# A transformer layer on eight cores: attention in half-row head units braided with its norms, no barriers, and a guarded second form of the softmax

## What is computed

```python
x = x + attn(layernorm(x))          # x: 8192 x 2048
x = x + ffn(layernorm(x))

def attn(q_in):                     # H=16 heads, D=128, M=1024 stored patterns per head
    proj = rms_norm(q_in, norm_query_w) @ W_in.T
    q = proj.reshape(B, S, H, D) @ W_q.T
    k = stored_patterns @ W_k.T
    v = stored_patterns @ W_v.T
    scores = einsum('bshd,hmd->bhsm', q * sigmoid(beta), k)
    out = einsum('bhsm,hmd->bshd', softmax(scores), v)
    return rms_norm(out.reshape(B, S, H * D), norm_retrieved_w) + q_in

def ffn(x):                         # 2048 -> 8192 -> 2048, int8 weights
    fuse = silu((x @ w_gate) * s_gate) * ((x @ w_up) * s_up)
    return (fuse @ w_down) * s_down
```

## Time and profile before

| | us |
|---|---|
| three runs | 2159.86, 2160.74, 2166.98 (median 2160.74) |
| span of the profiled execution, slowest core (6) | 2165.7 |
| spans of the eight cores | 2147.5 to 2165.7 |
| PE busy | 1804.8 (83%) |
| ACT / DVE / POOL busy | 607.3 / 240.3 / 146.6 |
| mean granted TensorE clock of core 6 | 0.891 |

### The profile page before, as it was taken

The page is one execution under the profiler, slowest core; times in us unless marked ns, Lnnn a source line. Parts: engine busy times, 40 slices in busy tenths (PEclk is TensorE's granted clock), DMA queues, the critical chain, the costliest instruction groups (busy, mean ns, idle before and its releaser), DMA issues.

```text
span 2165.7 us, 20546 instructions; the slowest of 8 cores (2147.5 to 2165.7 us)
## 1 busy us (share of the span) xinstructions
PE 1804.8 (83%) x8488; PEld 839.3 (39%) x8488; DVE 240.3 (11%) x455; ACT 607.3 (28%) x596; POOL 146.6 (7%) x239
## 2 busy tenths in 40 slices
PE   2349958888841499999999999999997979899695
PEld 2224433443421244444444444444443434344242
DVE  3530000000038300000000000000000020100202
ACT  1351156556656211111111111111113212222120
POOL 1000010000002100000000000000000010000101
PEclk9559958888865699999999999999998989999898
DMA  7610050000024222222222222222213131221301
GB/s 164 151 20 1 0 78 1 1 1 1 1 97 165 88 78 78 78 78 78 78 78 78 73 70 72 78 78 78 78 59 102 39 102 39 78 64 39 99 23 58
DMA packets 42367, 142.06 MB, mean 66 GB/s; under 512 B 6181, under 2 KB 6182, under 8 KB 38950
## 3 DMA queue, kind: packets, MB, share of 16 engines
q0 software_dynamic: 28592, 96.58, 15.4%
q1 hardware_dynamic: 13686, 44.19, 6.3%
HBM read 103.10 MB, written 16.78 MB: 55 GB/s over the span
## 4 chain that ended last, share of the span: by engine, by line
PE 78%; ACT 7%; DVE 6%; DMA 5%; issue 3%; POOL 0%; DVEq 0%; ACTq 0%; POOLq 0%; SPq 0%
PE PS L936 21%; PE PS L951 20%; PE PS L1076 19%; PE PS L462 5%; PE PS L547 3%; PE PS L562 2%; DMA out<-arena 2%; ACT arena L591 2%; PE PS L611 1%; DMA arena<-patT 1%; DVE arena L323 1%; PE PS L584 1%; PE PS L578 1%; ACT arena L439 1%; ACT arena L386 1%
## 5 line engine op out<-in xcount | busy, mean ns | idle before, releaser
L1076 PE MATMUL PS<-arena 128*128 128x512 bf16 x1956 | 451.9, 386 | 55.0 <-DVE arena L1015 44.3
L936 PE MATMUL PS<-arena 128*128 128x512 bf16 x2048 | 455.1, 381 | 5.6 <-DMA arena<-wu 5.6
L951 PE MATMUL PS<-arena 128*128 128x512 bf16 x1984 | 438.7, 379 | 0.0
L1076 PEld LDWEIGHTS PS<-arena 128*128 128x128 bf16 x1956 | 193.5, 99 | 298.1 <-issue 75.2
L936 PEld LDWEIGHTS PS<-arena 128*128 128x128 bf16 x2048 | 200.8, 98 | 249.2 <-issue 9.1
L951 PEld LDWEIGHTS PS<-arena 128*128 128x128 bf16 x1984 | 194.3, 98 | 234.0
L960 ACT ACTIVATE arena<-PS,sgc_s 128x1024 bf16<-128x1024 f32 x64 | 71.3, 1114 | 735.5 <-PE PS L945 735.5
L1043 ACT ACTIVATE arena<-arena 128x2048 bf16<-128x2048 int8 x64 | 121.8, 1908 | 351.7 <-PE PS L1065 342.0
L591 ACT ACTIVATE arena<-PS 128x1024 bf16<-128x1024 f32 x128 | 129.3, 1024 | 60.6 <-PE PS L578 60.6
L968 DVE TENSOR_TENSOR arena<-arena 128x1024 bf16<-128x1024 bf16 x64 | 44.3, 693 | 851.4 <-ACT arena L963 851.4
L462 PE MATMUL PS<-arena 128*128 128x512 bf16 x496 | 117.6, 391 | 8.2 <-ACT arena L439 8.2
(11 more groups left out here) (110 smaller groups left out, 927.4 us busy)
## 6 DMA issues: line engine op xcount, KB each, us to landing
arena<-wg POOLq DMA_DIRECT2D x64, 512.0 KB, 3.5
arena<-wu POOLq DMA_DIRECT2D x64, 512.0 KB, 4.2
arena<-x SPq DMA_DIRECT2D x16, 1024.0 KB, 5.2
arena<-wd SPq DMA_DIRECT2D x64, 256.0 KB, 2.6
arena<-win POOLq DMA_DIRECT2D x16, 512.0 KB, 6.8
x1sp<-arena SPq DMA_DIRECT2D x8, 1024.0 KB, 4.2
arena<-x1sp POOLq DMA_DIRECT2D x32, 256.0 KB, 5.1
out<-arena POOLq DMA_DIRECT2D x32, 256.0 KB, 3.5
```

What stands on the lines that cost most here:

```text
L936: En.matmul(PG[:, half * 512:half * 512 + 512], wgb[:, hc * 128:(hc + 1) * 128], x1nT3[:, hc, half * 512:half * 512 + 512], start=(hc == 0 ...
L951: En.matmul(PU2[:, half * 512:half * 512 + 512], wub[:, hc * 128:(hc + 1) * 128], x1nT3[:, hc, half * 512:half * 512 + 512], start=(hc == ...
L1076: En.matmul(PS[:, j * 512:(j + 1) * 512], fuse3[:, ic, j * 128:(j + 1) * 128], wdb[:, c * 512:(c + 1) * 512], start=(ic == 0), stop=(ic == ...
```

## The change

The whole layer is written anew; what PE multiplies in the feed-forward part stays.

- W_k and W_q are multiplied once into a 128x128 matrix with the factor sigmoid(beta) (L380), and keys are made with it (`kv`, L439). The fold, the query evacuation and the scaling by nqw as a pass of its own go.
- Attention runs over 32 slots (half of the rows hf, head h). In one slot's four positions p PE gets: two score matmuls of slot s, half of the projection of slot s+1 (p 0 and 1), a quarter of the keys and values of the next head, and 8 value matmuls of slot s-1 for one row tile. Values carry a column of ones (129 columns), so that the row sum comes out beside them and rows stay in partitions; the sum matmuls, the fp32 matmuls and the transposes of a head go.
- Norms are braided in: rows 4 to 7 of the first norm during slots 0 to 9 (`second_rows`); the second norm of the first half during the last ten slots, of the other half during the first gate/up items (`rows_g`). POOL applies the first norm and does small chains and products. Roots are by a bit trick and three Newton steps, on POOL or DVE.
- Gate/up items: 14 blocks for the first half of the rows, the same 14 for the second, then 50 for both. DVE reads the up part from PSUM itself.
- Down: weights are widened by the transfer (POOL queue), eight buffers deep; two last groups are taken bank by bank, so a bank ends every 8 matmuls; four output buffers, stores over SP.
- No barriers. A check adds up how many of the 1024 x 16 reciprocal row sums lie in [2^-60, 2^60]; each engine loads the flag at its end and branches. If any lies outside, the whole layer is done again in a second form with row maxima (`slow_attention`, `scores_max`).

```diff
-def barrier():
-nbar[0] += 1
-v = 3 * nbar[0]
-wait(Rt, cS, cS.n)
-wait(Rt, cV, cV.n)
...
-for R in (Rt, Rs, Rv):
-    wait(R, bar, v)
-bar.n = v
...
-           En.matmul(PSS[:, half * 512:half * 512 + 512], onemat[:],
-                     eT[:, m * 1024 + half * 512:m * 1024 + half * 512 + 512],
-                     start=(m == 0), stop=(m == MC - 1)))
...
-if g == 15:
-    for j in range(4):
-        I_x1re_load(q, j)
-    order = [(c, j) for j in range(NT) for c in range(4)]
-else:
-    order = [(c, j) for c in range(4) for j in range(NT)]
-for (c, j) in order:
-    ic = g * 4 + c
-    if q > 0 and ic == 0:
-        wait(Rt, cV, ep_j[q - 1][j])
...
+slots = [(0, h) for h in range(A_ONLY)]
+for h in range(A_ONLY, H):
+    slots += [(0, h), (1, h)]
+slots += [(1, h) for h in list(range(8, A_ONLY)) + list(range(8))]
...
+    t_nqs[j] = pool.tick(lambda En: En.tensor_scalar(ns[j % 2], xb[j % 4], r[:, 1:2], c[:, 0:1],
+                                                     ALU.mult, ALU.add), t_nb, t_x[j], nsfree[j % 2])
...
+            t = pe.tick(lambda En: En.matmul(bank(7, 128), wk, wq, start=True, stop=True), t_mats)
+            tg[0] = dve.tick(lambda En: En.tensor_scalar(gm, bank(7, 128), bsig[:, 0:1], None, ALU.mult),
+                             t, t_bsig)
...
+        if ec % 8 == 0:
+            pe.wait(*t_nqT[hf][ec])
...
+        t_pj[s] = dve.tick(lambda En: En.tensor_copy(pj[s % 2], bank(6)), t)
...
+        f = lambda En, i=i, mc=mc: En.matmul(bank(b + i), kT[:, h * M + mc * 128: h * M + (mc + 1) * 128],
+                                             pj[s % 2], start=True, stop=True)
...
+    t = act.tick(lambda En: En.activation(eT[s % 2][:, p * 1024:(p + 1) * 1024], bank(b, 1024), AF.Exp), t)
...
+    t = dve.tick(lambda En: En.tensor_reduce(warm[:, 0:1], bank(0, 1024), mybir.AxisListType.X, ALU.max),
+                 t, (act.sem, act.n))
...
+    t = act.tick(lambda En: En.activation(scratch, bank(0, 1024), AF.Exp, bias=warm[:, 1:2]),
...
+        f = lambda En, mc=mc: En.matmul(bank(b, 129, o),
+                                        eT[s % 2][:, mc * 512 + j * 128: mc * 512 + (j + 1) * 128],
+                                        v3[:, h * MC + mc, 0:129], start=(mc == 0), stop=(mc == MC - 1))
...
+        t = dve.tick(lambda En: En.reciprocal(r, u3[:, :, 128]), t)
+        t = dve.tick(lambda En: En.tensor_tensor(A3[:, j0:j0 + 2, h * 128:(h + 1) * 128], u3[:, :, 0:128],
+                                                 r.unsqueeze(2).to_broadcast([128, 2, 128]), ALU.mult),
...
+        tok[("w", c % 2)] = pool.tick(lambda En: En.tensor_tensor(aw[c % 2], A3[:, j, cs], wr[:, cs], ALU.mult),
+                                      t_A[hf], t_wr, tok.get(("s", c % 2)))
...
+        for j, p0 in zip(js, (5, 11, 19, 25)):
+            for c in range(8):
+                at(p0 - 1 + c // 2, lambda j=j, c=c: weighted(j, c))
+                at(p0 + c // 2, lambda j=j, c=c: summed_w(j, c))
+            for c in range(4):
...
+        for i, j in enumerate(js):
+            p0 = 6 + 6 * i
+            for c in range(4):
+                at(p0 + (0, 0, 2, 2)[c], lambda j=j, c=c: summed(j, c))
+                at(p0 + (3, 3, 4, 4)[c], lambda j=j, c=c: stats(j, c))
+            at(p0 + 5, lambda j=j: root(j, 1)())
+            at(p0 + 8, lambda j=j: x1n(j))
+            x1T_of(j, (p0 + 10, p0 + 12))
...
+    for s in range(NS):
+        hf, h = slots[s]
...
+        for p in range(4):
+            scores(s, p)
+            if s + 1 < NS and p < 2:
+                proj(s + 1, 8 * p, 8 * p + 8)
+            if nxt is not None:
+                kv(nxt, p, act if p % 2 else dve)
+            if s > 0:
+                values(s - 1, p)
+            for f in jobs.get((s, p), ()):
+                f()
+            while side and side[0][0] <= 4 * (s - (NS - A_ONLY)) + p:
+                side.pop(0)[1]()
...
+    side = rows_g(1, [6, 7], dve)
...
+items = [(ic, (0,)) for ic in range(N_HALF)] + [(ic, (1,)) for ic in range(N_HALF)]
+items += [(ic, (0, 1)) for ic in range(N_HALF, IC)]
...
+    t_wg[i] = (s_w[a].dma(pool, wb[a], wg_d[ic], *f0), s_w[b].dma(pool, wb[b], wu_d[ic], *f0))
...
+    t = dve.tick(lambda En: En.scalar_tensor_tensor(fuse[:, ic, c0:c0 + 512 * nh], bank(bu, 512 * nh),
+                                                    suc[:, ic:ic + 1], sg, ALU.mult, ALU.mult), t_u, t_s, t_cols)
...
+    t = dve.tick(lambda En: En.tensor_scalar(ok, rs[:], 2.0 ** -60, None, ALU.is_ge), pv_done[0])
+    tf[0] = dve.tick(lambda En: En.scalar_tensor_tensor(okb, rs[:], 2.0 ** 60, ok, ALU.is_le, ALU.mult), t)
...
+    t_flag[0] = dve.tick(lambda En: En.tensor_scalar(flag[0:1, :], PS[0:1, 7 * 512:7 * 512 + 1],
+                                                     float(NT * H * 128), None, ALU.not_equal), t)
...
+        item(i)
+        while side and side[0][0] <= 3 * i:
+            side.pop(0)[1]()
...
+        t_wd[g] = s_wd[g % 8].dma(pool, wdb[g % 8], wd_d[g // 16, g % 16], *toks)
...
+    t = dve.tick(lambda En: En.tensor_tensor(o, bank(j), sdt[:, q * 512:(q + 1) * 512], ALU.mult),
+                 t, t_sd, t_out.get(k - 4), h_end, *g_end)
+    bank_free[j] = [t]
+    t = dve.tick(lambda En: En.tensor_tensor(o, o, xr[k % 4], ALU.add), t, residual(k))
+    ep[k] = t
+    t_out[k] = s_out[k % 4].dma(sp, out_d[j][:, q * 512:(q + 1) * 512], o, t)
+    residual(k + 1)
+    load_xr(k + 4)
...
+for q in range(NQ):
+    for g in range(14):
+        pe.wait(t_wd[q * 16 + g], *[t_fuse[g * 4 + c] for c in range(4)])
...
+    pe.wait(t_wd[q * 16 + 14], t_wd[q * 16 + 15], *t_fuse[56:])
+    for k, j in enumerate(jorder):
+        for g in (14, 15):
+            for c in range(4):
+                if g == 15 and c == 3:
+                    t = pe.tick(down(q, g, j, c))
+                else:
+                    pe.do(down(q, g, j, c))
+        epilogue(q * 8 + k, t)
...
+    bad = En.value_load(flag[0:1, 0:1])
+    if i == 4:
+        for h, v in outs_fast:
+            En.wait_ge(h, v)
+    with En.If(bad != 0):
+        for f in slow[i]:
+            f(En)
+        if i == 4:
+            for h, v in outs_slow:
```

1735 lines of the change are left out of this document (749 added, 986 removed).

## The result

| | before | after |
|---|---|---|
| median, us | 2166.98 (2159.86 to 2184.01) | 1660.23 (1659.72 to 1661.46) |
| span of the profiled execution | 2165.7 | 1658.7 (core 1; all cores 1652.8 to 1658.7) |
| mean granted clock of that core | 0.891 | 0.994 |

After over before is 0.7652, with a 95% interval of 0.7601 to 0.7703. In two of the five runs of after (1798.8 and 1977.7 us) the cores of one die showed a lower clock; the table, and every median from here on, is of the undisturbed runs. The profiled execution is the one of 1660.23 us, so its span answers to the median within 1.6 us. Forecast were 1645 us, with a range of 1620 to 1705.

A forecast was written before the change was run, and what follows sets the result against it. PE was taken to bound the kernel, with time recoverable in the first five stages and down, not gate/up. Start 41, slots 254, gate/up 894, down 445 and end 11 sum to 1645 us, range 1620 to 1705.

The forecast's parts named there:

- slots: Attention slots up to gate/up: 238.4 us of matmuls at full clock plus 16 for hand-offs, 254 us.
- start: Up to the first scores: loads, first norm on POOL, transposes and first projection, 41 us (33 to 55).
- gate/up: Gate/up stage: 884.5 us plus last values, transposes and 4 us for weight traffic and no barrier, 894 us.
- down: Down stage: 442.2 us of matmuls plus 1 us per quarter end, 3 in all, 445 us.
- end: After the last matmul: two DVE steps, a store, the flag's load and the branch, 11 us.
- the signs named ahead: What would show it right, among others: first scores near 41 us, gate/up beginning near 295, down near 1189.
- Rival 1: Slots bound by hand-offs: a late copy stops PE and the clock falls; 1675 to 1765 us; chance 0.20.
- the hand-offs: In the slots, PE's losses waiting on other engines: 16 us taken, bounds 2 and 60.
- Rival 2: Transfers bound the start, up to slot 9: 15 to 35 us more, 1670; chance 0.14 together with rival 3.
- Rival 3: Second norm late in gate/up, half items wait for rows: 10 to 40 us more, 1670; chance 0.14 with rival 2.
- Rival 4: Faster than forecast: no hand-offs and transfers at full rate, 1616 us; chance 0.08.
- Rival 5: The second form runs, so the layer is done twice: near 4000 us, slower than before; chance 0.01.

The follow-up runs named there:

- actmove: The kernel after with squares moved earlier, norm passes in two halves, a root per row tile, transposes one or two positions behind: 1658.66 us (0.7691).
- best: The kernel after with squares in four roomy positions, halved norm passes, a root per row tile, tiles 3 and 4 earlier, norm weights late: 1652.12 us (0.7633).

## Why the prediction was right, and where it was off

**The sum.** 1645 us were forecast and the span is 1658.7. The slots took 25.3 us more than their term. The other four terms were all too high, by 1.0 (start), 3.5 (gate/up), 2.7 (down) and 4.4 (end), 11.6 together, and hid nearly half of that. So the closeness of the total is in part luck; the signs named ahead, gate/up beginning near 295 and down near 1189, came at 319.3 and 1209.8.

**What bounds.** Right. Stages 1 to 5 and the quarter ends were the recoverable part, and gate/up, with 5.4 us, was not.

**Start (41, measured 40.0).** Right in sum, from steps that partly offset. The fourth tile landed at about 24 us (25 were taken). The norm pass on POOL, for which no row existed, came in under both bounds: L331 takes 2.05 us, where the bounds were 2.35 and 6.4 and 3.5 was chosen. The lower bound was wrong, since I had taken it for granted that POOL can't beat DVE at one input. By the rule quoted there (the Trainium skill, GPSIMD Engine Reference, 4.1 Engine selection) the estimate was 1.7; the trace agrees with the rule better than with my choice. Its chains of small steps, the other blank, run at 0.34 us from start to start, 4 us for twelve. Rival 1 was right that DVE's steps behind them wait (3.13 us at 270.5); in the kernel after no stop of PE's as long as that follows from it, in `actmove` and `best` stops of 2.3 to 3.3 us did. The last steps of the start, from the chain:

```profile
28.81 2.05 POOL arena L331
...
30.99 1.03 PE PS L338 x8
...
32.11 1.24 DVE arena L353
...
33.48 5.63 PE PS L480 x16
...
39.21 0.70 DVE arena L489
...
40.04 0.59 PE PS L501 x2
```

**Slots (254, measured 279.3).** The matmul count was right; a slot without keys runs at 7.1 us where 7.0 were worked out, since eight value matmuls take 0.47 us, 0.059 each and not 0.056 (3 us in all). **The term that was mis-sized is the hand-offs: 16 taken, 41 measured**, inside the bounds of 2 and 60. 16 of the 41 are the second norm's, and 7 to 8 of these are ACT's. I added up ACT's exps and key copies, found 5.3 us of 7.9, and then looked at DVE for the norm and never at ACT, though the last ten slots give it eight squares (1.05 and 0.19 us) and four norm passes (2.10 us): 18.3 us in 88. That sum still fits. What counts is the length of a piece: 3.3 us in front of an exp or of transposes, where a position of a slot lasts 0.9 us without a projection in it. The other 25 lie in the earlier slots and in the pace: 5.6 us of waits for a key copy on DVE (L464), 3.5 for patT and 1.7 of lower clock behind it, 3 for the pace of the values, 5.3 in single waits (4.9 for DVE, 0.4 for ACT). That makes 19; 6 are spread over gaps that no row of a wait holds, and stay open.

**Gate/up (894, measured 890.5).** Right. Only 0.7 us of PE's time goes to a wait for weights, and the products of DVE keep up; "falls behind by 2 us" was not seen by PE at all.

**Down (445, measured 442.3) and end (11, measured 6.6).** Right, and the reserves of 3 and 1.5 us weren't needed. The single runs confirm both parts (16 us and 25 to 30 us when undone; 65 when put into the kernel before, with the order of the banks). The conversion through the transfer costs PE nothing: wd lands in 3.5 us, and PE has no wait in this stage.

**The rivals.** Rival 1 had the right place and a fraction of its size: 25 us more instead of 60 to 115. Rival 2 was half right: the DMA engines were nearly full for the first 75 us, but PE waited for them once, 3.5 us. Rival 3 did not happen in gate/up. Rival 4 would have wanted hand-offs of nearly nothing; the schedule `best` above is nearer to it by 7 us. Rival 5 didn't occur, and costs 2557 us (4215.5 - 1658.7), where 864 + 115 + 1340 = 2319 were worked out. Its slots took 196 us more than that, its norm 14, and its start, 43.7 us, had no term.

## What to carry to other kernels

When work is laid beside a stream of matmuls, budget each helping engine twice: the sum over the stretch, and the longest single piece in front of anything the matmuls need, which must fit between two such needs. Do so for every engine that the new work touches, also the one that looked idle. To find which engine is short, make one engine's pieces short with all waits kept and look at the time; moving them at first only showed other waits of the same size. That goes for every engine, POOL here among them, which PE's own list of waits does not name. And quarter ends are cheap to mend: more work per bank when banks are emptied, enough output buffers for a store, and a next quarter that asks for its banks one after another gave 65 us without the rest of the rewrite.

## What was unexpected in the hardware

- POOL takes 2.05 us for 128x2048, fp32 in and bf16 out, with one tensor input; DVE's 2.35 us for 128x2048 with two is slower. With two inputs POOL takes 0.68 us for 128x256.
- A load of a flag and a branch over a second copy of the whole program on each of five engines cost 0.1 us, which is within the noise.
- Two stops of PE of 2.7 and 3.1 us, 5 us apart, were followed by half clock (1.2 GHz), which showed in the matmuls between them and for some 5 us behind the second. In `actmove` one stop of 2.31 us (before 300.01) was followed by half clock too, from 300.4 us on, while in the kernel after one of 2.45 us (before 274.37) left the next 3 us at full pace. From 75 to 270 us, with five stops of 1.0 to 1.4 us, about 9 us or more apart but for one pair, it stayed at 1.00.
- A store of 256 KB took 5.8 us (median; 5.1 to 7.0 in the experiments that keep four) with four output buffers and 4.3 us with two.
